# Self- and cross-attention of a four-layer decoder: scores in both orientations, value mixing feature-major

## What is computed

```
q, k, v = xn @ Wq.T + bq, src @ Wk.T + bk, src @ Wv.T + bv     # xn = layernorm(x); src = xn or ctx
att = softmax(scale * q @ k^T (+ causal mask or relative bias), over keys)
x = x + (att @ v) @ Wo.T + bo
```

## Time and profile before

| | before |
|---|---|
| median of 3 runs | 6692.12 us (6683.45 to 6700.07) |
| span of the profiled execution | 6675.9 us |
| PE matmul busy, whole span | 4614.4 us (69%) |
| DVE busy | 4665.1 us (70%) |
| ACT busy | 2851.2 us (43%) |
| POOL busy | 1266.0 us (19%) |
| mean granted TensorE clock | 0.786 |

### The profile page before, as it was taken

The page is one execution under the profiler, slowest core; times in us unless marked ns, Lnnn a source line. Parts: engine busy times, 40 slices in busy tenths (PEclk is TensorE's granted clock), DMA queues, the critical chain, the costliest instruction groups (busy, mean ns, idle before and its releaser), DMA issues. The chain is left out here.

```text
span 6675.9 us, 127425 instructions
## 1 busy us (share of the span) xinstructions
PE 4614.4 (69%) x34862; PEld 3721.9 (56%) x34862; DVE 4665.1 (70%) x14726; ACT 2851.2 (43%) x6537; POOL 1266.0 (19%) x1740
## 2 busy tenths in 40 slices
PE   6878885335688777644777878405877777757888
PEld 5767773123577666632566666303555666646666
DVE  6778878532677788879898777633336778777766
ACT  5655551001455444433565664101225654436642
POOL 0000000176000011100000000057880002220000
PEclk9987776655677555556898999757998989879989
DMA  2000000333100011100000000122431000000000
GB/s 67 0 2 9 8 7 25 74 59 57 26 0 0 11 19 19 20 13 0 0 0 2 10 10 18 21 65 68 73 66 26 0 3 10 9 5 0 0 0 25
DMA packets 336231, 137.79 MB, mean 21 GB/s; under 512 B 179920, under 2 KB 326112, under 8 KB 335792
## 3 DMA queue, kind: packets, MB, share of 16 engines
q1 hardware_dynamic: 295168, 95.63, 5.9%
q0 software_dynamic: 40960, 40.93, 3.9%
HBM read 92.36 MB, written 43.86 MB: 20 GB/s over the span
## 5 line engine op out<-in xcount | busy, mean ns | idle before, releaser
L395 PE MATMUL ps<-vblock,probT 128*128 128x36 f32 x9216 | 1346.7, 298 | 4.5 <-ACT probT L532 4.0
L395 PEld LDWEIGHTS ps<-vblock,probT 128*128 128x128 f32 x9216 | 1339.8, 223 | 12.8 <-issue 9.2
L360 POOL TENSOR_TENSOR rstd<-vareps,half_power 128x1 f32<-128x1 f32 x576 | 316.1, 549 | 3638.9 <-DVE vareps L699 3638.9
L543 ACT ACTIVATE kblock<-ps,key_bias,key_scale 128x128 f32<-128x128 f32 x2304 | 869.0, 473 | 0.0
L439 PE MATMUL ps<-consts,prob 128*128 128x128 f32 x4608 | 795.9, 329 | 11.9 <-issue 5.4
L532 ACT ACTIVATE probT<-ps 128x512 f32<-128x512 f32 x1152 | 646.7, 596 | 169.5 <-PE ps L439 150.9
L439 PEld LDWEIGHTS ps<-consts,prob 128*128 128x128 f32 x4608 | 638.8, 169 | 79.1 <-issue 50.1
L413 PE MATMUL ps<-consts,o 128*128 128x128 f32 x512 | 184.0, 359 | 703.8 <-DVE vblock L640 329.3
L413 PEld LDWEIGHTS ps<-consts,o 128*128 128x128 f32 x512 | 75.5, 148 | 952.2 <-DVE vblock L640 467.7
L550 ACT ACTIVATE prob<-prob 128x1024 f32<-128x1024 f32 x512 | 550.8, 1076 | 57.4 <-DVE prob L757 38.2
L483 PE MATMUL ps<-kblock,qT 32*64 32x256 f32 x9216 | 448.9, 449 | 24.6 <-issue 9.4
(11 more groups left out here) (284 smaller groups left out, 8745.4 us busy)
## 6 DMA issues: line engine op xcount, KB each, us to landing
ctxT<-in_ctxT SPq DMA_DIRECT2D x256, 64.0 KB, 1.8
held<-in_g_w SPq DMA_DIRECT2D x16, 836.0 KB, 4.7
table<-prob SPq DMA_DIRECT2D x32, 256.0 KB, 2.3
x_dram<-x_res SPq DMA_DIRECT2D x16, 512.0 KB, 6.4
x_res<-x_dram SPq DMA_DIRECT2D x16, 512.0 KB, 7.2
x_res<-in_x SPq DMA_DIRECT2D x8, 512.0 KB, 7.2
x_res<-in_e_w SPq DMA_DIRECT2D x64, 64.0 KB, 1.8
z_dram<-o SPq DMA_DIRECT2D x128, 32.0 KB, 2.5
```

The source lines that it names most:

```text
L360: nc.gpsimd.tensor_tensor(k.rstd[:, par, 0:1], k.vareps[:, par, 0:1], k.half_power[:, 0:1], ALU.pow).then_inc(k.rstd_done, 1)
L395: mm = nc.tensor.matmul(k.ps_o[:, 2 * VW * j:2 * VW * (j + 1)], k.probT[:, b, j * P:(j + 1) * P], k.vblock[:, b, j, :, :].rearrange("p b c ...
L543: nc.scalar.activation(k.kblock[:, 1 - par, h, :], k.ps_k, ACT.Identity, scale=k.key_scale[:, a, h:h + 1], bias=k.key_bias[:, a, h:h + 1]) ...
```

## The change

All nine attention stages are rewritten; the other stages keep their work. Buffers come in threes, the loop runs three steps a pass, the depth of the pipeline goes from 5 to 7 steps (11 in L1_xattn, 9 in L3_xattn), and each stage allocates its own semaphores and clears them behind an all-engine barrier.

- Scores are computed twice: with queries on partitions (`s1`, only for the row maximum) and with keys on partitions (`s2`, 32 matmuls of 64 columns), so that no probability is transposed.
- The row maximum (128 x 16, spread to 128 columns) is transposed once and subtracted inside PSUM by 32 matmuls whose weights are constants of -1 (`less_max`). ScalarE takes the exponential straight from PSUM.
- Masks and the relative bias are added in PSUM by matmuls with an identity, into both score layouts; two transposed bias tables are built.
- Mixing has weights of 64 rows by 32 columns (`vblock`: four heads of 8 columns, all but one head's zero) and 64 moving columns; row sums come from 32 more matmuls with weights of ones. The result is already feature-major, so one reciprocal and one multiply of 128 x 128 give `oT`.
- `kblock` is built by one GpSimd multiply of 128 x 512, the normalised `xn` by ScalarE, the output bias is added by GpSimd.

TensorE's part of a step, cut to its core:

```diff
+    def query_scores(buf, groups):
+        for g in groups:
+            rows = slice(32 * g, 32 * g + 32)
+            for b in range(2):
+                mm = nc.tensor.matmul(
+                    k.s1[S * b:S * b + S, g % 2, (g // 2) * GH * S:(g // 2 + 1) * GH * S],
+                    k.qT[rows, buf, S * b:S * b + S], k.kblock[rows, buf, :, S * b:S * b + S],
+                    start=not added, stop=not added or groups == high, tile_position=(32 * g, S * b))
+        return mm
...
+    def less_max(buf, h, groups):
+        for g in groups:
+            rows = slice(32 * g, 32 * g + 32)
+            for b in range(2):
+                mm = nc.tensor.matmul(
+                    k.s2[S * b:S * b + S, g % 2, (g // 2) * GH * S + h * S:(g // 2) * GH * S + (h + 1) * S],
+                    k.consts[rows, C_PICK + S * h:C_PICK + S * h + S], k.mT[rows, buf, S * b:S * b + S],
+                    start=False, stop=groups == high and h == GH - 1, tile_position=(32 * g, S * b))
+        return mm
...
+    def mix(weights, col, buf, h, b):
+        rows = slice(S * b, S * b + S)
+        for g in range(GROUPS):
+            at = head_pos(g, h)
+            lhsT = (k.vblock[rows, buf, 32 * (GH * g + h):32 * (GH * g + h) + 32] if weights == "values"
+                    else k.consts[rows, C_ONES + 32 * h:C_ONES + 32 * h + 32])
+            mm = nc.tensor.matmul(k.ps_o[32 * g:32 * g + 32, b, col:col + S], lhsT, k.probT[rows, buf, at:at + S],
+                                  start=h == 0, stop=h == GH - 1, tile_position=(S * b, 32 * g))
+        return mm
...
+            nc.tensor.matmul(k.ps_q, wq, k.xnT[:, b2, :], start=True, stop=True)
+            mm = nc.tensor.matmul(k.ps_k, wk, k.ctxT[:, b2, :] if cross else k.xnT[:, b2, :], start=True, stop=True)
...
+            pe.wait_ge(k.xn_done, upto(it, 1, ends))
+            mm = nc.tensor.transpose(k.ps_xT, k.xn[:, b1, :], k.ident)
...
+            if added:
+                for c in range(2):
+                    nc.tensor.matmul(k.s1[:, c, :], pick, added_to_queries(c), start=True, stop=False)
...
+        if score1:
+            mm = query_scores(b3, low)
+        if score2:
+            for h in range(GH):
+                mm = key_scores(b4, h, high, first=not added)
...
+                nc.tensor.matmul(k.ps_y, k.oT[:, b6, :], wo, start=True, stop=True).then_inc(k.y_psum, 1)
...
+        if score1:
+            query_scores(b3, high).then_inc(k.s1_psum, 1)
+        if score2:
+            for h in range(GH):
+                mm = key_scores(b4, h, low, first=False)
...
+        for h in range(GH):
+            if score2 and softmax:
+                mm = less_max(b4, h, low)
+            if mixes:
+                mix("values", 0, b5, h, 1)
...
+            nc.tensor.matmul(k.ps_v, k.ctxT[:, b3, :] if cross else k.xnT[:, b3, :], wv, start=True,
+                             stop=True).then_inc(k.v_psum, 1)
...
+        for h in range(GH):
+            if score2 and softmax:
+                mm = less_max(b4, h, high)
+            if mixes:
+                last = mix("values", 0, b5, h, 0)
+        if score2 and softmax:
+            mm.then_inc(k.s2_psum, 1)
+        if mixes:
+            if softmax:
+                for h in range(GH):
+                    for b in range(2):
+                        last = mix("ones", S, b5, h, b)
+            last.then_inc(k.o_psum, 1)
```

`low` is head groups 0 and 1 (array rows 0 to 63), `high` groups 2 and 3; `key_scores` is `query_scores` with the operands exchanged, one head at a time. The other engines' new instructions:

```diff
+            nc.gpsimd.tensor_tensor(k.kblock[:, buf, :, :], kT, masks, ALU.mult).then_inc(k.kblock_done, 1)
...
+            nc.scalar.activation(k.probT[:, b4, :], k.s2.rearrange("p c n -> p (c n)"), ACT.Exp).then_inc(
+                k.guard_done if name == "L1_xattn" else k.exp_done, 1)
...
+            nc.scalar.activation(k.xn[:, par, :], stream[:, bass.ds(it * P, P)], ACT.Identity, scale=k.rstd[:, par, 0:1],
+                                 bias=k.nmr[:, par, 0:1]).then_inc(k.xn_done, 1)
...
+            nc.vector.tensor_reduce(spread, heads, AX.X, ALU.max).then_inc(
+                k.max_raw if name == "L1_xattn" else k.max_done, 1)
...
+                nc.vector.reciprocal(inv, k.ps_o[:, :, S:2 * S]).then_inc(k.inv_done, 1)
...
+            nc.vector.tensor_tensor(k.oT[:, b5, :].rearrange("p (b q) -> p b q", b=2), k.ps_o[:, :, 0:S], inv,
+                                    ALU.mult).then_inc(k.on_done, 1)
+    tile_pipeline(dve, step, depth_of(name), unroll=NB)
```

More of the change, by code:

```diff
@@ L49 @@
 POST_NORM = {"L1_xattn": 0, "L3_xattn": 1}
-BIASED = {"L0_xattn", "L1_attn", "L2_attn", "L3_xattn"}
+QUERY_BIAS = {"L0_xattn", "L1_attn", "L1_xattn", "L3_attn", "L3_xattn"}
+KEY_BIAS = {"L0_xattn", "L1_attn", "L1_xattn", "L3_xattn"}
+VALUE_BIAS = {"L0_xattn", "L1_attn", "L1_xattn", "L3_attn", "L3_xattn"}
+MASK_ROWS = {"L0_xattn": 0, "L2_attn": 1}
 C_ID, C_HEAD, C_CAUSAL, C_FUTURE, C_UPPER = 0, 128, 132, 196, 260
@@ new lines, in depth_of, with post_back, upto, wait @@
+def depth_of(name):
+    return {"L1_xattn": 11, "L3_xattn": 9}.get(name, 7)
+def post_back(name):
+    return {"L1_xattn": 8, "L3_xattn": 6}[name]
+def upto(it, back, ends, count=TILES):
+    if ends is None:
+        return it - back + 1
+    return max(0, min(count, it - back + 1))
+def wait(eng, sem, value):
+    if positive(value):
+        eng.wait_ge(sem, value)
+def fronts(name, it, ends):
+    last = TILES + (1 if name == "L3_xattn" else 3)
+    return it if ends is None else min(last, it)
@@ L333, in step @@
             for b in range(2):
-                sp.dma_start(k.z_dram[bass.ds((it - 3) * P + S * b, S), :]
+                sp.dma_start(k.z_dram[bass.ds((it - 6) * P + S * b, S), :]
                               .rearrange("s c -> (s c)").rearrange("(h q d) -> q h d", h=HEADS, d=HD),
[L336 to L345, removed]
@@ L559, in attention_act, with added_to_queries, added_to_keys @@
-    tile_pipeline(act, step, depth_of(name))
-def attention_dve(k, dve, name, n):
+    wq, wk, wv, wo = (k.attn_w[:, a, m, :] for m in range(4))
+    cross = name in CROSS
+    softmax = name != "L3_xattn"
+    added = name in MASK_ROWS or name == "L1_attn"
+    low, high = (0, 1), (2, 3)
+    pick = k.ident if name == "L1_attn" else k.ident_bf[:, :]
+    def added_to_queries(c):
+        return k.relpos[:, 512 * c:512 * c + 512] if name == "L1_attn" else k.mask_rows[:, MASK_ROWS[name], 0, :]
+    def added_to_keys(c):
+        return k.relposT[:, 512 * c:512 * c + 512] if name == "L1_attn" else k.mask_rows[:, MASK_ROWS[name], 1, :]
@@ new lines, in barrier @@
+    def barrier():
+        nc.tensor.matmul(k.ps_y[:, 0:1], k.ident, k.ident[:, 0:1], start=True, stop=True)
+    def query_scores(buf, groups):
[7 more added lines that the diff above has]
+        return mm
@@ new lines, in key_scores @@
+    def key_scores(buf, h, groups, first):
+        for g in groups:
[3 more added lines that the diff above has]
+                    k.s2[S * b:S * b + S, g % 2, (g // 2) * GH * S + h * S:(g // 2) * GH * S + (h + 1) * S],
+                    k.kblock[rows, buf, h, S * b:S * b + S], k.qT[rows, buf, S * b:S * b + S],
+                    start=not softmax or (first and h == 0), stop=not softmax, tile_position=(32 * g, S * b))
+        return mm
@@ L580, in post_norm_stats, with attention_dve, post_sums @@
+def attention_dve(k, dve, name):
+    nc = k.nc
+    a = ATTENTIONS.index(name)
+    softmax = name != "L3_xattn"
+    stream = k.held if name == "L3_ffn" else k.x
+    def post_sums(it, par, ends):
+        back = post_back(name)
+        buf = (par - back) % NB
+        post, kept = k.post[:, buf, :], k.held[:, bass.ds((it - back) * P, P)]
+        dve.wait_ge(k.held_done, upto(it, back, ends))
+        wait(dve, k.post_done, upto(it, back + 3, ends))
         if name == "L1_xattn":
-            dve.wait_ge(k.z_loaded[buf], 8 * (t - buf + 2))
@@ L1376, in shared_pass @@
     w_quad = k.r_w if choose else k.r_score
[L1377 removed]
+    hidden = k.wide if FC > 1 else k.halves
     with nc.Block() as block:
```

917 lines of the change are left out of this document (434 added, 483 removed).

## The result

The changed kernel takes **9425.3 us** (median of 4 runs, 9398.3 to 9435.0) against 6696.1 for the kernel before (4 runs): a ratio of 1.406, 95% interval 1.403 to 1.409. It is slower by 41%, where 6145 was forecast. The profiled execution has a span of 9424.2 us.

The account below looks back on a forecast made before the run. It took a ring TensorE, VectorE, TensorE as the bound. Plain tile: 5.15 us at full clock, 5.5 with the clock's ratio. Stages -682, resets +27, constants +5, code +100: 6145 us; own range 5750 to 6450, 5750 to 7700 with rival 1.

Parts of the forecast that it names:

- Two stretches of 32 `less_max` and 32 mixing records: TensorE, plain tile: the two kinds overlap on opposite halves of the array, 8 records a piece, 0.50 us each, 1.00.
- Rival 1: `less_max` and mixing: each change between two piece shapes stops the array, 0.25 us a group, total 7655 us; chance 0.30.
- rival 2: TensorE's clock falls to 0.58 as small pieces count as less work, +1480 us, 7600; chance 0.07.
- I take 0.6 a pass, +100: TensorE's loop code: 0.6 exposed loads at each of 9 x 18 passes, 1.8 us each; bounds 0 and 290 us.
- front: TensorE, plain tile: q and k 0.45, two transposes 0.21, change back to the full array 0.11; 0.77 us.
- the bursts: TensorE, plain tile: two bursts of 8 query and 32 key score records on small pieces, 2 x 0.61 = 1.22 us.
- both projections: TensorE, plain tile: output projection with change and exposed load 0.40 us, values projection 0.50.
- row sums: TensorE, plain tile: 64 records on 8 pieces, 0.45 us.
- The price of 0.056 us for a 64-column record on its piece: TensorE, small pieces: time taken for each 64-column record, from about 0.24 us for the second 256-column record on a piece.
- Rival 3: Handing over does not shrink: `kblock` at its ceiling, ring ScalarE, GpSimd, ScalarE late, plain tile near 6.4, about 6500 us; chance 0.10.
- The cover of 1.15 us: Path around TensorE: row sums and next q and k cover 1.15 of 1.6 us from last maxima to next transpose, leaving 0.45.
- the 27 us for resets and barriers: Nine resets with a barrier, 3 us each, between 1 and 5: +27 us.

Follow-up runs that it names:

- e1: Changed kernel, same TensorE instructions grouped by shape of array piece, 7 changes of shape a tile instead of 20; 7531.8 us, ratio 1.128.
- e3: Changed kernel with `less_max` and value mixing alternating by half groups, 36 changes of shape a tile instead of 20; 12432.2 us, ratio 1.861.
- e7: e4 with the output and values projections each written three times over in L3_xattn alone; 6413.7 us, ratio 0.954.
- e6: e4 with mixings and row sums ahead of `less_max`, and ScalarE's normalisation ahead of its exponential; 6677.4 us, ratio 0.993.
- e5: Changed kernel in its own order, head mask also on the queries, key scores in 8 matmuls of 256 columns instead of 32 of 64; 8015.9 us, ratio 1.193.
- e4: e1 with e5's edit, and `less_max` as 8 matmuls of 256 columns instead of 32, VectorE spreading the maxima; 6495.2 us, ratio 0.967.

## Why the prediction was wrong

**The step that failed** is the line "Two stretches of 32 `less_max` and 32 mixing records, on opposite halves of the array. If they overlap: 8 records a piece, 0.50 each, 1.00." They do not overlap at all. At full clock the eight pairs take 4.16 us, at half 6.3 (8 x 0.79). Rival 1 had the mechanism and the unit price: 0.25 us a group at full clock, measured 0.26. The argument against it, that small pieces in different rows do not hold each other up, was read from the earlier trace rows, where all pieces have one shape; it says nothing of two shapes. The Trainium skill (TensorEngine Tiling (Array Packing), Key Properties) has it right: a change of the tiling mode drains the engine. e1 and e3 show it with the same instructions, 7532, 9425 and 12432 us for 7, 20 and 36 changes a tile. Rival 1's own total, 7655, was still 1770 too low, since it took the clock's old ratio (6.83 to 6.41) and 100 us for the code.

**The clock** (rival 2, 0.07) was half right. Work on small pieces can hold a high clock: e1's L3_attn has 0.92 with the records of the changed kernel. It falls where more changes of shape or code loading stop TensorE, and then each stop lasts longer as well. That the stops alone bring it down is not shown: the kernel before stood a fifth of its time in the plain stages and had 0.90 to 0.93, and L1_attn of e1, with 83 packets and its fp32 full-array matmuls, had 0.95. Stops and the lower share of full-array work come together in all runs but e7. In L3_xattn, where TensorE has mostly small pieces, it was 0.50 in the changed kernel and in e1 to e6, with TensorE up to 98% busy, and 353 us forecast became 500; e7 shows that full-array work raises it. The kernel before had 0.88 there with TensorE only 78% busy. The forecast asked how long TensorE's work is at full clock and took the clock as given; the two are one question.

**Code.** "I take 0.6 a pass, +100", with 0 to 290 as bounds, was too small by far. Both its parts were: not one block a pass but about 9, and not 1.8 us but 3.7 to 4.9. It is worth some 1.5 us a tile in five stages at the slow order (480 us, from e5's difference of means; the stops seen are 1.1 to 1.4), and with the clock at least some 2.3 a tile in three stages of e1; from e1 to e4 1037 us are gained in all. The Trainium skill (Runtime: NRT & Kernel Launch, Instruction fetch mechanics) gives 2048 instructions for TensorE. The prediction's conclusion from it, that a body of some 1800 just fits, is not borne out here: such a body was loaded anew in five stages and, moved by half a block, in seven. Bodies shorter by 288 instructions (e5: 3 steps, 48 records each, a weight load and a matmul apiece) stayed loaded in all nine.

**TensorE's other prices** were low too. Against e1's tile: front 0.86 (0.77 forecast), the bursts 0.96 and 0.75 (0.61 each), both projections 0.84 (0.90), and in grouped order `less_max` and value mixing 2.08 (1.00), row sums 0.83 (0.45). In all 6.3 instead of 4.4 without the wait. The price of 0.056 us for a 64-column record on its piece nearly holds for `less_max` (31 spacings in 0.48 us over 4 pieces: 0.062), not for the 64x32 pieces of mixing (128 records in 1.40 us over 8 pieces: 0.088).

**What held.** The reciprocal of 128 columns, 0.96 forecast, 0.958; `kblock` 1.3 taken, 1.04; the exponential 1.08 and 1.02. VectorE took 3.3 us a plain tile (212.9 over 64; 3.4 forecast), ScalarE 2.5 (2.9), GpSimd 2.4 (2.8): all stayed covered. Rival 3 (handing over) is not seen: TensorE's wait for `xn` is 177 us over nine stages, 0.3 a tile. L1_attn was to go from 544 to 609 us; it took 1008, and 549 with order and code mended (e4), without its drain.

**Readings that do not add up.** The cover of 1.15 us in "The path around it" is not the sum of its two terms: row sums and q and k are 0.45 each there, 1.01 with the change of shape. VectorE in L1_xattn comes to 7.5 us a tile by the items named (8.3 less 1.6 plus 0.8), not 6.9; it measured 6.1. The 1.75 us in front of L413 is the weight loader's; the matmuls stand 1.30 there, which is the 1.3 that the sum subtracts. No run shows the 27 us for resets and barriers apart from the rest. None of these decided the outcome.

**What stays open.** Which alignment lets a body of some 1750 instructions stay loaded, and the exact split of the 2729 us: each stop costs more at a lower clock, so the shares of order, code and clock do not simply add. By runs, order alone gives back 1893, the shorter body after it 1037, and e4 is then 222 us faster than the kernel before (6717 beside it).

## What to carry to other kernels

Count the changes between shapes of array pieces before counting columns: put all matmuls of one shape in a row, since here each change cost 0.13 us at full clock and about 0.22 at half, and the overlap within its group as well. Read the granted clock next to the busy share for every stage, and reckon that a stop of TensorE may be paid twice, by its length and by the clock; a stage that stays at 0.50 while busy may run faster with more full-array work. Keep the body of an unrolled TensorE loop near the 1460 instructions that stayed loaded here (about 1750 did not always), and look at the instruction queue's packets per pass: the stages that stayed loaded had at most about one, those that did not had four to nine.

## What was not expected of the hardware

- More work made a stage faster: 8 extra full-array records a tile, 6.47 to 5.29 us, clock 0.50 to 0.94 (e7).
- VectorE's 512-column multiply for `mblock`, both inputs in SBUF, takes 0.68 us when GpSimd's multiplies do not run beside it and 1.31 us when they do (medians of 73 and 439 in e4); in L3_attn of e6, where it runs ahead of them, it is 0.68. The Trainium skill (SBUF — State Buffer, Who interferes with whom) says that a VectorE instruction with two SBUF inputs contends with GpSimd's reads; the trace agrees. GpSimd's own goes from 1.04 to 1.49 us at times.
